# A graph kernel's adjacency matrix is kept once, and the two transposed passes turn its tiles on the way in

## What is computed

```python
for i in range(3):                                   # layer 0: GRU
    m = h @ weight[i]
    agg = segment_sum(m[src], dst)                   # A^T-like product, three times
    h = gru_cell(agg, h, ...)
# layer 1: hypergraph convolution
e_feat = B_inv * segment_sum(h[row], col)            # one direction
out    = D_inv * segment_sum(e_feat[col], row)       # the other direction
# layer 2: attention
e = leaky_relu(s1[src] + s2[dst])
out = segment_sum(softmax_over_src(e) * mapped[dst], src)   # the other direction
# layer 3: an MLP per edge, gathered row by row (no matrix)
```

## Time and profile before

| | us |
|---|---|
| median of three runs | 5899.56 |
| lowest and highest | 5891.83, 5899.86 |
| profiled execution | 5895.11 |
| its span | 5893.0 |
| PE busy in the span | 4074.7 (69%) |
| DVE, ACT, POOL busy | 2255.1, 1685.4, 2578.0 |

### The profile page before, as it was taken

The page is one execution under the profiler, slowest core; times in us unless marked ns, Lnnn a source line. Parts: engine busy times, 40 slices in busy tenths (PEclk is TensorE's granted clock), DMA queues, the critical chain, the costliest instruction groups (busy, mean ns, idle before and its releaser), DMA issues. The chain is left out here.

```text
span 5893.0 us, 80722 instructions
## 1 busy us (share of the span) xinstructions
PE 4074.7 (69%) x24696; PEld 3170.2 (54%) x24698; DVE 2255.1 (38%) x4547; ACT 1685.4 (29%) x2823; POOL 2578.0 (44%) x2583
## 2 busy tenths in 40 slices
PE   4960000000999998996999799679999577777777
PEld 2430000000787787874555455369999466666665
DVE  5993000000446446437000100547777633333333
ACT  0020000000555555543000100358877322222222
POOL 0037777777777777760000000000000377777772
PEclk9985555555999999998999899799999799999998
DMA  5929500000883883881666666114543111111111
GB/s 188 407 77 366 209 0 0 0 3 0 275 285 102 274 271 106 286 233 41 195 200 173 160 200 199 44 57 144 148 143 116 43 52 50 51 51 51 50 51 39
DMA packets 307968, 786.87 MB, mean 134 GB/s; under 512 B 100762, under 2 KB 116823, under 8 KB 307783
## 3 DMA queue, kind: packets, MB, share of 16 engines
q1 hardware_dynamic: 182152, 548.50, 30.2%
q10 hardware_dynamic: 43680, 177.21, 7.8%
q0 software_dynamic: 81952, 58.72, 4.5%
HBM read 599.36 MB, written 184.70 MB: 133 GB/s over the span
## 5 line engine op out<-in xcount | busy, mean ns | idle before, releaser
L548 POOL DMA_INDIRECT rows<-table,idx_ring x880 | 871.7, 991 | 2291.2 <-ACT idx_ring L556 2023.4
L1017 POOL DMA_INDIRECT adj_t<-cell_val,cell_at x832 | 811.7, 976 | 637.4 <-DVEq L1705 362.1
L1017 POOL DMA_INDIRECT adj_s<-cell_val,cell_a x832 | 871.0, 1047 | 281.5 <-issue 281.5
L450 PE MATMUL ps<-tiles_r,stage_r 128*128 128x512 f32 x1524 | 605.0, 397 | 285.3 <-ACT tiles_r L406 280.5
L406 ACT CAST tiles_r<-onehot 128x1024 fp32r<-128x1024 f16 x254 | 266.6, 1050 | 1260.3 <-DMA onehot<-adj_t 1065.0
L452 PE MATMUL ps<-tiles_r,lower_r 128*128 128x512 f32 x1524 | 602.5, 395 | 0.0
L1405 PE MATMUL ps<-ident,big 128*128 128x128 f32 x14 | 3.2, 425 | 714.1 <-DVE big L1813 714.1
L459 PE MATMUL ps<-big,onehot 128*128 128x387 bf16 x2695 | 461.6, 329 | 47.8 <-DMA onehot<-adj_s 42.6
L459 PE MATMUL ps<-big 128*128 128x387 bf16 x2695 | 459.0, 328 | 42.7 <-DMA big<-adj_t 39.1
L597 PE MATMUL ps<-rows,ident 128*128 128x128 f32 x1760 | 397.2, 310 | 131.6 <-DMA rows<-table,idx_ring 99.5
L450 PEld LDWEIGHTS ps<-tiles_r,stage_r 128*128 128x128 f32 x1524 | 290.4, 191 | 354.4 <-issue 281.6
(11 more groups left out here) (355 smaller groups left out, 6491.4 us busy)
## 6 DMA issues: line engine op xcount, KB each, us to landing
onehot<-adj_t SPq DMA_DIRECT2D x338, 512.0 KB, 4.5
big<-adj_t SPq DMA_DIRECT2D x338, 512.0 KB
onehot<-adj_s SPq DMA_DIRECT2D x170, 512.0 KB, 3.6
adj_t<-rows ACTq DMA_DIRECT2D x13, 6656.0 KB, 46.8
adj_s<-rows ACTq DMA_DIRECT2D x13, 6656.0 KB, 53.8
big<-adj_s SPq DMA_DIRECT2D x84, 512.0 KB
x_fm<-adj_s SPq DMA_DIRECT2D x84, 512.0 KB
rows<-table,idx_ring POOLq DMA_INDIRECT x880, 2.5
```

Of the source, the lines that this page charges most:

```text
L450: nc.tensor.matmul(psum_fm(p, n)[:, 0:cut], upper_rows[:, k, :], tile[:, 0:cut], start=k == 0, stop=False, skip_group_check=True)
L548: nc.gpsimd.indirect_dma_start(rows[:, s, 0:P], None, table[0:N, :], bass.IndirectOffsetOnAxis(idx_ring[:, s:s + 1], 0),).then_inc(row_lan ...
L1017: nc.gpsimd.indirect_dma_start(out, bass.IndirectOffsetOnAxis(cells[:, c:c + 1], 0), cell_val[:, c:c + 1], None).then_inc(S(f"{name}{2 * c ...
```

## The change

`adj_s` is gone, with its zeroing, its scatters, its addresses and SP's wait for it. Passes 4 and 5 (`FLIPPED` = 4 and up) take their tiles from `adj_t`. The tile for group g and turn t is taken from the rows of group t and the columns of group g, turned by the DMA: `load_flipped` issues four transposing transfers, each reading 128 rows of 512 cells (1 KB a row) and writing four blocks of 128 by 128 cells. All four raise the slot's semaphore, so `landed` counts 64 a tile in place of 16.

```diff
+FLIPPED = 4
...
-        cell_a2 = sb("cell_a2", [P, EC], I32)
...
-        adj_s = dram("adj_s", (CELLS + P * EC, 1), F16)
...
+        def load_flipped(tile, g, t, landed_on):
+            out = tile.rearrange("p (m j c) -> p m j c", m=KT, j=KT)
+            for j in range(KT):
+                cells = adj_t[bass.ds(t * P * ROW, P * ROW), :].rearrange("(p c) a -> p (c a)", c=ROW)
+                nc.sync.dma_start_transpose(out[:, :, j, :], cells[:, bass.ds(g * TW + j * GW, GW)]).then_inc(landed_on, 16)
...
-                    sp.dma_start(raw_tile(p, s), tiles[bass.ds(g * P, P), t * TW:(t + 1) * TW]
-                                 ).then_inc(tile_landed[s], 16)
+                    if p >= FLIPPED:
+                        load_flipped(raw_tile(p, s), g, t, tile_landed[s])
+                    else:
+                        sp.dma_start(raw_tile(p, s), tiles[bass.ds(g * P, P), t * TW:(t + 1) * TW]
+                                     ).then_inc(tile_landed[s], 16)
...
-            for q in range(2):
-                sp.wait_ge(S(f"as_written{q}"), 16 * EC // 2)
-            sp.wait_ge(S("as_ext"), 16 * EXT_BLOCKS)
             matrix_sp(4, sp)
...
-            pool.wait_ge(S("cells_ready"), 4)
+            pool.wait_ge(S("cells_ready"), 3)
             scatter_ext(adj_t, 16, "at_ext")
-            pool.wait_ge(S("as_zero"), 16 * GROUPS)
-            pool.wait_ge(S("cells_ready"), 3)
-            for c in range(EC):
-                scatter_cells(adj_s, cell_a2, "as_written", c)
-            scatter_ext(adj_s, 20, "as_ext")
             edge_pool(pool)
...
-            for g in range(GROUPS):
-                zero_cells(act, adj_s, g, "as_zero")
-            act.wait_ge(S("as_zero"), 16 * GROUPS)
...
-            cells(cell_a2[:, :], src_s, col_v)
-            dve.sem_inc(S("cells_ready"), 1)
```

More of the change, by code:

```diff
@@ L275, in S @@
             return made[name]
-        row_landed = [Count(S(name), 16 * EC // 2) for name in ("at_written0", "at_written1", "as_written0", "as_written1")] + \
-            [Count(S(f"row_landed{s}"), 0) for s in range(4, 2 * CH)]
+        row_landed = [Count(S(name), 16 * EC // 2) for name in ("at_written0", "at_written1")] + \
+            [Count(S(f"row_landed{s}"), 0) for s in range(2, 2 * CH)]
         TURNED = ["_h0x", "_hy", "_hr", "_x2", "_x3"]
@@ L365, in raw_tile @@
             return (raw_att if MODES[p] == "att" else raw_big)[s]
+        def load_flipped(tile, g, t, landed_on):
[3 more added lines that the diff above has]
+                nc.sync.dma_start_transpose(out[:, :, j, :], cells[:, bass.ds(g * TW + j * GW, GW)]).then_inc(landed_on, 16)
         def matrix_sp(p, sp):
-            tiles = (adj_t if p < 4 else adj_s)[0:CELLS, :].rearrange("(r c) a -> r (c a)", c=ROW)
+            tiles = adj_t[0:CELLS, :].rearrange("(r c) a -> r (c a)", c=ROW)
             def body(n, g, first_turn, i):
@@ L384, in landed @@
             turn = first_turn + t
-            eng.wait_ge(tile_landed[turn % RING], 16 * (turn // RING + 1) + 16 * (STEP // RING) * i)
+            plain = PASS_TURNS * FLIPPED
+            at_first = 16 * (turn // RING + 1)
+            if turn >= plain:
+                at_first += 16 * (KT - 1) * len([n for n in range(plain, turn + 1) if n % RING == turn % RING])
+            eng.wait_ge(tile_landed[turn % RING], at_first + 16 * (KT if turn >= plain else 1) * (STEP // RING) * i)
         def matrix_act(p, act):
@@ L1796, in _ @@
             step(nc.vector.tensor_tensor(ext_i[:, 16:19], node_ai, node_bi, ALU.bitwise_or))
[L1797 to L1802, removed]
             dve.sem_inc(S("cells_ready"), 1)
```

## The result

The changed kernel takes 6620.92 us in the median of four runs, against 5899.08 us: a ratio of 1.1227, 95% interval 1.1207 to 1.1246. The forecast was 5910 us with a range up to 6560, so the time lies beyond the range, on the side that the in-between rival named. Its profiled execution has a span of 6617.2 us, 724.2 more than before.

The account below looks back on a forecast made before the run. The prediction took TensorE to bound the GRU passes, with loads hidden. Removed work 0, pace of pass 4 +5 and first tiles +5 us made +10 us on the median of 5899.56: 5910 us, range 5890 to 6560.

Parts of the forecast that it names:

- in-between rival: TensorE's wait for tiles in passes 4 and 5: engine work stretches loads, 6070 us at 3.6 us a tile, 6540 at 5; chance 0.27.
- (e): SP's issue of tile loads: four at the plain 0.332 us, 1.33 us a tile, hidden until one holds SP 0.66 us.
- (g): First tile of passes 4 and 5, which nothing hides: 1 to 4 us each, taken 2.5, together 5 us.
- (f): DMA engine time per transposed tile: between 1.71 and 2.7 us, costing pass 4 5 us of a possible 12.
- the far bound: DMA engines in passes 4 and 5: every 256-byte block row its own piece, 6.4 us a tile, 7010 us; chance 0.14.
- The 46 ns floor: DMA engines: least time per piece, read off degree_row's 6,656 pieces of 4 bytes, plus a part growing with size.
- the 63 ns of x_in: DMA engines: time per 512-byte piece, read off x_in's load taken as 6,144 pieces.
- the 85: DMA engines: 85 ns per 1 KB row, from a straight line between 63 and 214 ns, giving 2.7 us a tile.
- (a) to (d): Removed second scatter, zeroing, VectorE's address steps and SP's wait before pass 4: together 0, at most 5 us gained.
- the two stretch to the same time per group: Sign in the next profile: passes 4 and 5 slow to one equal pace, so the load alone sets both.
- One transfer at a time: Loads in passes 4 and 5: four serial landings of 2.1 us, 8.4 us a tile, 7690 us; chance 0.07.
- The faster rival: Removed traffic had slowed the GRU passes and first scatter by more than seen, visible in L450's pace: 5885 us; chance 0.04.

Follow-up runs that it names:

- experiments 8: The changed kernel with one transposing transfer of 128 x 2048 cells a tile in place of four: 5856.1 us, ratio 0.9922 to the kernel before.
- Experiments 10: The kernel before with only the first half of the second scatter (416 of 832 instructions): 5899.4 us, ratio 1.0000 to the kernel before.
- 12: The kernel before with only the first half of the second scatter, run again in another group: 5898.44 us, ratio 0.9993 to the kernel before.

## Why the prediction was wrong, step by step

- **(e) issue on SP.** This step failed. The sum priced a transposing issue like a plain one, 0.332 us, and named 0.66 us as the point from which it would show; it measured 1.19 us, and 1.31 with the pause. Four are 5.24 us a tile. The point was right and the price was wrong by a factor of 3.6, in a place to which I gave no rival of its own. All but some 7 of the 772 us of the two passes follow from it: with one issue a tile, 2.2 us, the two passes take 7 us more than before, near the 5 us of (g).
- **(f) DMA engine time.** Bounds of 1.71 and 6.4 us, taken below 2.7; measured 2.5 us. The value was right for a wrong reason: the transfer does go in 256-byte pieces, as the far bound had it, but a piece takes 18 ns, not the 50 read off the x_in and degree_row rows. So it was luck that the value held. The 46 ns floor was that of other transfers, and the 63 ns of x_in were misread: its 6,144 rows of 512 bytes are not so many pieces. The rows of SP's queue, in 2625 to 2660 us of the trace of before and in 2611 to 2632 us of the changed kernel's, say:

```profile
q1 hardware_dynamic: 1660, 3.20, 62.3%
...
q1 hardware_dynamic: 1660, 3.20, 54.5%
```

These are 1,660 pieces of some 2 KB: 0.623 x 35 x 16 / 1,660 = 210 ns each before and 0.545 x 21 x 16 / 1,660 = 110 ns after; the stretch before was also disturbed, as the next point but one tells. A line from 46 ns to 110 ns at 2 KB still gives about 80 ns at 1 KB, so the 85 came out by chance. 524,288 bytes in 2.5 us are 210 GB/s. The Trainium skill's 261 GB/s (DMA: Bandwidth & Descriptors, Latency and other measured facts) would be an estimate of 2.0 us a tile; the measured rate is 20% lower and decides, and it does not change what hides.
- **(g) the first tiles.** Priced at 2.5 us a pass. TensorE started pass 4 after a wait of 45.6 us in place of 42.6, 3 us more, within the 1 to 4. The stage rows of the table show more, since the first group then runs at the slow pace.
- **(a) to (d), the removal.** Priced at 0 to -5 us; measured -13 by pass 0, -15 between passes 2 and 3, and -18 behind pass 5. I had looked only at the pace within the passes, and that is as unchanged as I said, 23.98 us a group. That comparison could not say what I took from it, as both groups lie before the scatter's end at 2631 us and none runs without it; experiments 8 and 10 show the 24.0 us without. The first part: some 4 us are the zeroing, which lengthened a gap of GpSimd at 520 us from 3 to 7 us. About 3.7 us of longer scatters stand in the trace of before at 381 to 393 us, beside the 14 dropped steps of VectorE; that this is contention was not tried. A further 4 us are a second longer gap, at 671 us, which did not come back with the zeroing and stays open. The second part is the wait for x_in, before and after:

```profile
DVE x_nm L1835 <- DMA x_nm<-x: 21.9, 1, 21.9
...
DVE x_nm L1829 <- DMA x_nm<-x: 5.1, 1, 5.1
```

x_in was issued at 2625.69 us, and the last scatter at 2631.4 us. Experiments 10 and 12 moved the end of the scatter into pass 1 and the stall went with it, so something at the end of the second scatter, not its running, stalls the transfers beside it by 10 to 17 us. What it is was not told apart: the last three scatters are those of `scatter_ext`, which landed 14 to 25 us after their issue in the trace of before and 2.1 us into `adj_t`, and the moment is also that at which GpSimd stops issuing. The third part, in the edge stage, goes along with gathers of 979 ns in place of 991 (880 of them: 11 us); its cause is open.
- **The rivals.** The in-between rival gave 6540 us at 5 us a tile, close to the time, with the mark "the two stretch to the same time per group", which came true. But it placed the cost in the engines' work, and that was wrong: the share of 0.46 excludes it. One transfer at a time is excluded by landings of 2.7 us with an issue each 1.31. (Its 2.1 us was no plain load but a scatter of `scatter_ext`; the shortest landing of a plain load is 3.4 us.) The faster rival, 5885 us, was right about removed traffic costing something, 48 us of it, but not in L450's pace, where it looked.
- **The slower condition.** Nothing in the trace before could show that a load may wait for 16 scatters, and that removing the second scatter is worth 1068 to 1079 us. There the change was faster, 0.9578. Which sign the change has depends on the condition, and nothing in the prediction could say so.

## What to carry to other kernels

Price a new kind of transfer twice, for the engines that move it and for the sequencer that issues it, and ask of both whether they fit in the time of the step that hides them; here bytes, pieces and landing all fitted and the issue did not. A price per issue that hardly grows with the transfer is paid back by making the transfer larger, even if the reader must follow another order in the slot. Before turning a matrix, see whether it is its own transpose. Count a queue's pieces in the trace and not in the source, before a time per piece is read off it. And look at where a background stream of transfers ends and at what else is issued there, not only at the pace while it runs.

## What the hardware showed that was not expected

- A transposing issue held SP for 1.15 us (128 x 128 cells of two bytes), 1.19 us (128 x 512), 1.23 us (128 x 1024) and 1.82 at the least, 2.2 us in the median (128 x 2048), a plain load of 512 KB for 0.33 us.
- A 256-byte piece of a transposing transfer took a DMA engine 18 ns; a tile of 512 KB took the 16 engines 2.5 us, against 1.71 us plain.
- With 128-cell indirect scatters running on GpSimd's queue, plain loads of SP moved 280 GB/s in one trace and 21 GB/s in another, one 512 KB load per 16 scatters. The same kernel takes 5896 to 5899 us or 7302 to 7355 us, and one chip gave both at different times. What brings the condition was not tried and stays open.
- At the end of the second scatter the transfers beside it landed late, and the work behind them lost 10 to 17 us, in three traces and at two places of that end.
